# Image 0 in three transfers, TensorE sums part of the first cells, another split of tile 0

## The chip, the cores and the metric

The kernel runs on one core of one Trainium2 chip. Its time is the device time of one launch, in microseconds (us). A core has five engines with a queue of instructions each: TensorE (PE in the rows; PEld is its weight load), VectorE (DVE), ScalarE (ACT), GpSimd (POOL) and SyncE (SP), which here only issues DMA. They meet by semaphores.

## The reference

32 images of 96 channels, 56 by 56, fp32. The first layer scales every channel of every image by a gain that is computed from the data, the second is a depthwise masked 3x3 convolution whose four taps (left-up, up, right-up, left) are computed from the result of the first.

```python
# layer 0 (cut): which frequency each channel takes, from image 0 alone
g = relu(bn2(einsum('nchw,oc->nohw', x, wg1))).mean(axis=(2, 3))
xg0 = (relu(tanh(g @ wg2.T + bg2)) + beta)[0]
p_mid = round(xg0[:31] / xg0.sum() * 96)      # -> param, the edges of 32 channel ranges
filt = basis[i] where param[i] <= channel < param[i + 1]
# gain of each (image, channel): sums over a grid of 7 x 7 cells of 8 x 8 pixels
xp = x.reshape(n, c, 7, 8, 7, 8).mean(axis=(3, 5))
y = relu(bn1(sum(xp * filt) @ w1d[:, :, 1].T + b1d))
x = x * y[:, :, None, None] + x
# layer 1 (cut)
t = relu(bn(x.mean(axis=(2, 3)) @ w1.T))
wt = (t @ w2.T + b2).reshape(n * 96, 1, 3, 3) * mask   # 4 taps are left
out = depthwise_conv(x, wt, padding=1) + bias
```

## The kernel before

A tile is 128 rows (one image and channel each) of 3136 numbers; a group of three tiles is four whole images, and there are 8 groups, 24 tiles. SyncE loads tiles into nine buffers `xin` and stores them from four buffers `xout`. Tile k+9 is loaded when tile k has been computed.

**Steady state.** The rows of a tile are split among engines. VectorE computes the upper 27 rows (`tap`, three passes for the taps left-up, right-up and left; the tap up and the bias come with the seed, `seed_d` on ScalarE). TensorE computes the lowest 11 rows (`array_taps`, three products with the diagonal matrices `diag`) and two of the taps of the 18 rows between (`mixed_taps`); VectorE adds the last tap of those (`finish_mixed`, line 569). ScalarE seeds the sums, makes the diagonals and copies the 11 rows out. GpSimd does the left column of the result and folds a later tile to an eighth, which VectorE then sums to 49 cells. A product of TensorE in fp32 stands as two records in the trace. Beside this the coefficients of the next group are computed: `weigh_cells` on VectorE, then in turn `mix`, `hide`, `make_taps` and `spread_taps` on TensorE, with small steps of ScalarE and VectorE between them, and `coef_steps` at the end.

**Head.** Nothing can be convolved before the coefficients of group 0 are there. Three things lead to them, in this order on the engines:

1. The gate, from image 0. Its pixels come once more by DMA, into `image0` (a part of `xout`), in a layout of four quarters of 32 partitions each, by four transfers (line 287). `gate_w` holds the weights four times on its diagonal; GpSimd clears it and VectorE copies the blocks in (line 408). TensorE multiplies (line 698, six products of 392 columns), ScalarE applies batch norm and relu and sums (line 604), then a small product (701), tanh (607), `xg` (500), its sum (704), `counted` (507), `bounds` (707, 511), `hit` (515), `later` (710), `chosen` (521), `chosen_rows` (610) and the product `filt` (713) follow.
2. The cells of tiles 0, 1 and 2. VectorE reduces them directly (`sum_direct`, line 435) between the steps of the gate; GpSimd first folds 4 of the 7 cell rows of tile 1 and 3 of tile 2 in half (line 342, behind `counted`), and VectorE reduces the halves (line 442).
3. `weigh_cells(0)` (lines 464 to 470), then mix (721, 723), lift (619), total (477), hide (729), hidden (624), make_taps (735), gained (482), spread_taps (742) and `coef` (489, 494). VectorE reduces tile 3 in three pieces between them. Then it seeds its own rows of tile 0 (line 542), and the steady state begins.

`warm` (line 685) and line 689 are products with zeros; the former fill in where TensorE would stand still, the latter are needed once for each bank pair that is accumulated into. Lines 314 to 325 end the kernel with the stores of the last tile.

Of the kernel before, what the change touches and what calls it, by code (L numbers as in the profile page):

```python
# [33 lines left out]
VECTOR_ROWS, MIXED_ROWS, ARRAY_ROWS = 27, 18, 11  # L34
TOP_B = VECTOR_ROWS
TOP_A = VECTOR_ROWS + MIXED_ROWS
CHUNK_A = (ARRAY_ROWS + 1) // 2
CHUNK_B = (MIXED_ROWS + 1) // 2
BANK_A, BANK_B, BANK_D, BANK_S = 0, 2, 4, 7

# [3 lines left out]
HEAD_FOLDED = (0, 4, 3)  # L44
# [22 lines left out]
W_BIAS = 0  # L67
W_MIX = W_BIAS + PER
W_HIDE = W_MIX + PER * C
W_IDENT = W_HIDE + HID  # L70
W_IMAGE = W_IDENT + P
# [19 lines left out]

def build(nc, x, early, narrow, wide, out):
# [7 lines left out]
    x_image0 = x[0, :, :, :].rearrange("c h w -> c (h w)").rearrange("(q t) (j f) -> j q t f", t=PER, j=GROUP)  # L100

    with ExitStack() as ctx:
# [11 lines left out]
        gate_one = sb("gate_one", [QUAD, PER, E_END])  # L114
# [16 lines left out]
        edges = sb("edges", [P, 3, TOP_A])  # L131
# [34 lines left out]
        w_hid = wide_sb[0:C, W_HIDE:W_IDENT]  # L166
        ident = wide_sb[:, W_IDENT:W_IMAGE]
# [7 lines left out]
        acc_a = banks[:, BANK_A:BANK_B, :].rearrange("p b f -> p (b f)")[:, BANK - CHUNK_A * W:BANK + (ARRAY_ROWS - CHUNK_A) * W]  # L175
        acc_b = banks[:, BANK_B:BANK_D, :].rearrange("p b f -> p (b f)")[:, BANK - CHUNK_B * W:BANK + (MIXED_ROWS - CHUNK_B) * W]
        acc_d = banks[:, BANK_D:BANK_S, :].rearrange("p b f -> p (b f)")[:, 0:VECTOR_ROWS * W]
        gate_out = banks[:, BANK_A:BANK_B, :].rearrange("p b f -> p (b f)")[:, BANK - GATE_HALF:BANK + GATE_HALF]
        small = banks[:, BANK_S, :]
# [41 lines left out]
        image0_in = [sem(f"image0_in_{j}") for j in range(GROUP)]  # L221
# [4 lines left out]
        gate_zeroed = sem("gate_zeroed")  # L226
# [641 lines left out]
```

## Time and profile before

| | |
|---|---|
| median of three runs | 226.35 us (226.28 to 226.87) |
| profiled execution | 225.73 us, of which the span from first to last instruction is 223.9 us |
| busy: PE / DVE / POOL / ACT | 199.2 / 196.4 / 147.2 / 128.9 us |
| moved | 79.08 MB, 353 GB/s over the span |
| first tap of tile 0 | 36.0 us after the start |
| mean granted TensorE clock | 0.953 of 2.4 GHz |

All times in the rows count from the start of the span. The span has two parts: a head of 36 us, in which the engines wait for each other in a chain, and a steady part of 24 tiles at about 7.6 us, in which VectorE and TensorE are busy nearly all the time. The granted clock is 1.00 (2.4 GHz) in the steady part and changes between 1.00 and 0.50 (1.2 GHz) in the head.

### The profile page before, as it was taken

How to read it: one execution, taken by the hardware profiler on the slowest of the kernel's cores; microseconds unless marked ns; L12 is line 12 of the kernel's file. 1: busy time of each engine (PE TensorE's matmuls, PEld its weight loads, DVE VectorE, ACT ScalarE, POOL GpSimd, SP SyncE). 2: the span in 40 equal slices, each digit the busy share in tenths (PEclk: the TensorE clock that was granted, in tenths of full speed). 3: DMA queues.
4: the chain of work that ended last, by engine and by line, in shares of the span. 5: the costliest groups of instructions: out<-in, count | busy, mean ns of one | idle time of the engine just before them, and what ended most of it. 6: DMA issues, size and time to landing. Idle time of an engine off the chain costs nothing.

```text
span 223.9 us, 2408 instructions
## 1 busy us (share of the span) xinstructions
PE 199.2 (89%) x742; PEld 119.7 (53%) x742; DVE 196.4 (88%) x216; ACT 128.9 (58%) x190; POOL 147.2 (66%) x139
## 2 busy tenths in 40 slices
PE   7291775999999999999999999999999999999990
PEld 3141463556556565656664666466646654765540
DVE  6036969999999999999999999989999999988983
ACT  2002115638766867676867685768576857687640
POOL 3004267999999999999999999998999500040000
PEclk9769585999999999999999999999999999999999
DMA  4999999949999999999999999999997336625685
GB/s 112 279 426 418 430 428 425 395 155 332 421 426 405 419 426 426 408 397 430 430 422 408 428 426 428 408 423 426 423 406 325 148 143 287 287 108 215 254 332 241
DMA packets 8157, 79.08 MB, mean 353 GB/s; under 512 B 1040, under 2 KB 1072, under 8 KB 2128
## 3 DMA queue, kind: packets, MB, share of 16 engines
q1 hardware_dynamic: 8144, 78.92, 86.5%
q8 instruction: 6, 0.10, 0.2%
q14 instruction: 7, 0.06, 0.1%
HBM read 40.38 MB, written 38.54 MB: 352 GB/s over the span
## 4 chain that ended last, share of the span: by engine, by line
DVE 47%; PE 34%; issue 7%; ACT 5%; DMA 3%; SPq 1%; DVEq 1%; ACTq 0%
DVE banks L560 23%; PE banks L750 23%; DVE xout L560 8%; DVE xout L569 7%; PE banks L698 3%; ACT banks L635 3%; DMA xout<-x 3%; PE banks L735 2%; PE banks L742 2%; DVE stats L442 2%; DVE sums L467 1%; PE banks L685 1%; DVE stats L448 1%; DVE stats L435 1%; DVE stats L464 1%
## 5 line engine op out<-in xcount | busy, mean ns | idle before, releaser
L750 PE MATMUL banks<-xin,diag 128*128 128x330 f32 (+2 forms) x480 | 162.5, 492 | 2.9 <-ACT banks L635 2.9
L750 PEld LDWEIGHTS banks<-xin,diag 128*128 128x128 f32 x480 | 89.5, 192 | 58.0 <-issue 36.6
L635 ACT ACTIVATE banks<-xin,wide_sb,coef 128x616 f32<-128x616 f32 (+2 forms) x71 | 84.4, 1208 | 21.3 <-DVE xout L560 10.7
L342 POOL TENSOR_TENSOR halves<-xin 128x1568 f32<-128x1568 f32 (+2 forms) x22 | 74.1, 3370 | 23.2 <-DVE count L507 14.7
L560 DVE SCALAR_TENSOR_TENSOR banks<-xin,coef,banks 128x1485 f32<-128x1485 f32 x48 | 84.8, 1767 | 4.8 <-ACT banks L635 4.2
L560 DVE SCALAR_TENSOR_TENSOR xout<-xin,coef,banks 128x1485 f32<-128x1485 f32 x24 | 42.2, 1758 | 0.6 <-issue 0.3
L347 POOL TENSOR_TENSOR halves<-halves 128x784 f32<-128x784 f32 x18 | 33.2, 1846 | 1.4
L569 DVE SCALAR_TENSOR_TENSOR xout<-xin,coef,banks 128x990 f32<-128x990 f32 x24 | 29.8, 1243 | 2.5 <-PE banks L750 2.5
L630 ACT ACTIVATE diag<-wide_sb,coef 128x128 f32<-128x128 f32 x72 | 23.4, 389 | 9.7 <-DVE coef L494 9.7
L656 ACT ACTIVATE xout<-banks 128x616 f32<-128x616 f32 x24 | 16.4, 682 | 17.6 <-PE banks L750 16.7
L374 POOL TENSOR_TENSOR edges<-xin,coef 128x90 f32<-128x90 f32 x24 | 8.3, 347 | 19.0 <-DVE coef L494 19.0
L352 POOL TENSOR_TENSOR rows<-halves 128x392 f32<-128x392 f32 x18 | 18.3, 1019 | 1.4
L435 DVE TENSOR_REDUCE stats<-xin 128x14 f32<-128x896 f32 (+3 forms) x9 | 11.0, 1227 | 7.7 <-DMA xin<-x 7.7
L698 PE MATMUL banks<-xout,gate_w 128*128 128x392 f32 x12 | 6.8, 747 | 4.1 <-DMA xout<-x 4.1
L448 DVE TENSOR_REDUCE stats<-rows 128x49 f32<-128x392 f32 x18 | 10.0, 554 | 0.0
L604 ACT ACTIVATE banks<-banks,b_gate,a_gate 128x784 f32<-128x784 f32 x1 | 1.0, 977 | 14.7 <-PE banks L698 14.7
L624 ACT ACTIVATE hidden<-banks,b_hid,a_hid 32x4 f32<-32x4 f32 x8 | 2.8, 346 | 11.4 <-PE banks L729 11.4
L735 PEld LDWEIGHTS banks<-hidden,narrow_sb 32*96 32x96 f32 x64 | 6.0, 159 | 5.6 <-issue 5.1
L721 PEld LDWEIGHTS banks<-by_image,wide_sb 128*96 128x96 f32 x48 | 5.0, 175 | 5.4 <-DVE by_image L470 4.2
L379 POOL TENSOR_TENSOR xout<-edges,wide_sb 128x45 f32<-128x45 f32 x24 | 6.6, 273 | 1.9
L377 POOL TENSOR_TENSOR edges<-edges 128x45 f32<-128x45 f32 x24 | 6.2, 260 | 1.9
L698 PEld LDWEIGHTS banks<-xout,gate_w 128*128 128x128 f32 x12 | 3.4, 297 | 7.5 <-issue 7.2
(73 smaller groups left out, 88.4 us busy)
## 6 DMA issues: line engine op xcount, KB each, us to landing
xin<-x SPq DMA_DIRECT2D x23, 1568.0 KB, 9.7
out<-xout SPq DMA_DIRECT2D x23, 1568.0 KB, 11.7
xout<-x SPq DMA_DIRECT2D x4, 294.0 KB, 5.1
xin<-x SPq DMA_DIRECT2D x1, 1120.0 KB, 14.5
out<-xout SPq DMA_DIRECT2D x1, 756.0 KB, 3.2
out<-xout SPq DMA_DIRECT2D x1, 504.0 KB, 3.3
wide_sb<-wide SPq DMA_DIRECT2D x1, 499.5 KB, 15.8
xin<-x SPq DMA_DIRECT2D x1, 448.0 KB, 15.1
```

The costliest lines, as they stand in the source:

```text
L342: eng.tensor_tensor(halves[:, j % 2, 0:end, :], cells[:, :, 0, :], cells[:, :, 1, :], ALU.add).then_inc(once_folded, 1)
L347: eng.tensor_tensor(cells[:, :, 0, :], cells[:, :, 0, :], cells[:, :, 1, :], ALU.add).then_inc(twice_folded, 1)
L352: eng.tensor_tensor(rows8[:, j % 2, :].rearrange("p (a f) -> p a f", a=DCT), cells[:, :, 0, :], cells[:, :, 1, :], ALU.add).then_inc(thric ...
L435: return vec.tensor_reduce(cells_of(j, first, end), xin[:, j % IN_BUFS, PAD + first * BLK * W:PAD + end * BLK * W].rearrange("p (a b c d) ...
L448: return vec.tensor_reduce(stats[:, 0, j % PER, :], rows8[:, j % 2, :].rearrange("p (c d) -> p c d", d=BLK), AX.X, ALU.add)
L560: return vec.scalar_tensor_tensor(out=to, in0=grid(k)[:, irows, cols], scalar=weight(k, which), in1=d_rows[:, :, ocols], op0=ALU.mult, op1 ...
L569: vec.scalar_tensor_tensor(out=result(k)[:, TOP_B:TOP_A, ocols], in0=grid(k)[:, irows, cols], scalar=weight(k, LEFT), in1=b_rows[:, :, ocols],
L630: ins = sca.activation(diag[:, k % 2, which, :], ident, ACT.Copy, scale=weight(k, which))
L635: return sca.activation(acc, above_rows(k, first, end), ACT.Identity, bias=bias[:, k % PER:k % PER + 1], scale=weight(k, UP))
L656: sca.activation(xout[:, k % OUT_BUFS, TOP_A * W:], acc_a, ACT.Copy).then_inc(a_out, 1)
L698: ins = mm(gate_out[:, part], gate_w[:, t, :], image0[:, t, part], start=(t == 0), stop=(t == PER - 1))
L750: return mm(to, diag[:, k % 2, which, :], grid(k)[:, irows, cols], start=False, stop=(which == LEFT), skip_group_check=True)
```

## The change

- **Image 0** comes in three transfers, one for each channel of three, each to all 128 partitions (a channel in four quarters on four neighbouring partitions). The first products wait only for the first transfer. `gate_w` is now made by three VectorE multiplications of the gate's weights, which come spread over 128 partitions, with a 0/1 matrix `quarter_of`; GpSimd's clearing and the four copies go.
- **Parameters.** `early_sb` and `narrow_sb` are issued by ScalarE, ahead of its table load. The array `wide` is split: its first 132 columns (`quarter_of` and `ident`) come ahead of image 0, the rest where all of it came before.
- **Cells.** TensorE adds the eight pixel rows of a cell row up, by eight accumulating products with the identity (`sum_cells`), for 4, 4, 3 and 2 of the 7 cell rows of tiles 0 to 3; VectorE reduces what is left, one eighth of the numbers (`sum_array`). Before, these were direct reductions in tiles 0 and 3 and reductions of halves in tiles 1 and 2. GpSimd's two folds of the head go. VectorE's direct sum of four cell rows of tile 0 ahead of `xg` goes.
- **TensorE's filling**: 4 products with zeros ahead of the gate where there was 1, 2 behind it, two for the second bank pair ahead of `s_mm`, 1 behind `s_mm`, 1 between mix and hide; the 2 ahead of mix go.
- **Tile 0** is split 20/18/18 rows. ScalarE seeds the array rows of tile 0 before it makes the diagonals, and each diagonal is signalled by itself. The sums of VectorE's rows start 8 numbers later in their banks.

```diff
+ROWS = (27, 18, 11)
+FIRST_ROWS = (20, 18, 18)
+ARRAY_CELLS = ((0, 4), (0, 4), (0, 3), (0, 2))
...
         def _(sp):
-            sp.dma_start(early_sb[:, :], early[:, E_GATE2:E_END]).then_inc(early_in, 16)
-            sp.dma_start(gate_one[:, :, :], early.rearrange("(q t) e -> q t e", t=PER)).then_inc(gate_one_in, 16)
-            for j in range(GROUP):
-                sp.dma_start(image0[QUAD * j:QUAD * (j + 1), :, :], x_image0[j]).then_inc(image0_in[j], 16)
-            sp.dma_start(narrow_sb[:, :], narrow).then_inc(narrow_in, 16)
+            sp.dma_start(gate_one[:, :], early.rearrange("(q j t) e -> q j (t e)", j=1, t=PER).broadcast_to(
+                [QUAD, GROUP, PER * E_END])).then_inc(gate_one_in, 16)
+            sp.dma_start(wide_sb[:, 0:W_BIAS], wide[:, 0:W_BIAS]).then_inc(ident_in, 16)
+            for t in range(PER):
+                sp.dma_start(image0[:, t, :], x_image0[t]).then_inc(image0_in[t], 16)
...
-            pool.wait_ge(loaded[1], 16)
-            pool.wait_ge(counted, 1)
-            fold_once(1, HEAD_FOLDED[1])
-            pool.wait_ge(part_in, 16)
-            fold_once(2, HEAD_FOLDED[2])
...
-            dve.wait_ge(loaded[0], 16)
-            sum_direct(0, 0, 4)
             dve.wait_ge(gate_tanh, 1)
             vec.tensor_scalar(xg[:, :], gate_act[:, :], 0.0, gate_par[0:NF, 5:6], ALU.max, ALU.add).then_inc(xg_done, 1)
-            sum_direct(0, 4, 5)
...
+            sum_array(0).then_inc(cells_done, 1)
+            dve.wait_ge(loaded[1], 16)
+            sum_direct(1, 4, DCT)
+            sum_array(1).then_inc(cells_done, 1)
             dve.wait_ge(part_in, 16)
-            sum_direct(2, HEAD_FOLDED[2], HEAD_PART)
+            sum_direct(2, 3, HEAD_PART)
             dve.wait_ge(loaded[2], 16)
             sum_direct(2, HEAD_PART, DCT)
-            sum_once_folded(2, 2, HEAD_FOLDED[2]).then_inc(cells_done, 1)
+            sum_array(2).then_inc(cells_done, 1)
...
+            def sum_cells(j, begin, stop):
+
+                first, end = ARRAY_CELLS[j]
+                cells = xin[:, j % IN_BUFS, PAD:].rearrange("p (a b f) -> p a b f", a=DCT, b=BLK)
+                for b in range(begin, stop):
+                    ins = mm(array_cells_of(j), ident, cells[:, first:end, b, :],
+                             start=(b == 0), stop=(b == BLK - 1))
```

On TensorE, from its first instruction to the sum of `xg` (`prime` is L689 and L746, `warm` L685 and L730, the gate L698 and L756). Before:

```order
L689 MATMUL banks<-zeros 128x512 x2
L685 MATMUL banks<-zeros 128x392
L698 MATMUL banks<-xout,gate_w 128x392 x6
L701 MATMUL banks<-gate_sum,gate_in 32x1
L704 MATMUL banks<-xg,narrow_sb 32x1
```

and in the changed kernel:

```order
L746 MATMUL banks<-zeros 128x512 x2
L730 MATMUL banks<-zeros 128x392 x4
L756 MATMUL banks<-xout,gate_w 128x392 x6
L730 MATMUL banks<-zeros 128x392 x2
L760 MATMUL banks<-gate_sum,gate_in 32x1
L746 MATMUL banks<-zeros 128x512 x2
L764 MATMUL banks<-xg,narrow_sb 32x1
L730 MATMUL banks<-zeros 128x392
```

Three more wide products with zeros stand ahead of the gate, two behind it, and two ahead of the sum of `xg`.

On TensorE, from `bounds` to mix. Before:

```order
L707 MATMUL banks<-count,narrow_sb 32x1 x2
L710 MATMUL banks<-hit,narrow_sb 32x96
L713 MATMUL banks<-narrow_sb,chosen_rows 128x49 x3
L685 MATMUL banks<-zeros 128x392 x2
L721 MATMUL banks<-by_image,wide_sb 96x4 x3
L723 MATMUL banks<-by_image,wide_sb 96x4 x3
```

and in the changed kernel, where L737 is `sum_cells`:

```order
L768 MATMUL banks<-count,narrow_sb 32x1 x2
L737 MATMUL banks<-xin,wide_sb 128x224 x3
L773 MATMUL banks<-hit,narrow_sb 32x96
L737 MATMUL banks<-xin,wide_sb 128x224 x5
L777 MATMUL banks<-narrow_sb,chosen_rows 128x49 x3
L737 MATMUL banks<-xin,wide_sb 128x224 x8
L737 MATMUL banks<-xin,wide_sb 128x168 x8
L785 MATMUL banks<-by_image,wide_sb 96x4 x3
L787 MATMUL banks<-by_image,wide_sb 96x4 x3
```

The products `later` (L773) and `filt` (L777) now stand behind 3 and 5 wide ones in the same queue, and mix behind 16.

On TensorE, from hide to the products of tile 0. Before:

```order
L729 MATMUL banks<-total,wide_sb 32x4
L735 MATMUL banks<-hidden,narrow_sb 96x4 x4
L742 MATMUL banks<-taps,wide_sb 128x16 x3
L750 MATMUL banks<-xin,diag 128x6x55 x3
L750 MATMUL banks<-xin,diag 128x5x55 x3
```

and in the changed kernel:

```order
L730 MATMUL banks<-zeros 128x392
L793 MATMUL banks<-total,wide_sb 32x4
L737 MATMUL banks<-xin,wide_sb 128x112 x3
L799 MATMUL banks<-hidden,narrow_sb 96x4 x4
L737 MATMUL banks<-xin,wide_sb 128x112 x2
L806 MATMUL banks<-taps,wide_sb 128x16 x3
L737 MATMUL banks<-xin,wide_sb 128x112 x3
L814 MATMUL banks<-xin,diag 128x9x55 x10
```

The cells of tile 3 stand in three pieces between the narrow products, and the products of tile 0 are 9 rows each.

## Rows read from the trace of the kernel before

**Rows 1.** Chain that ended last, in order of time: start us, us, what.

```profile
3.65 6.23 DMA xout<-x
...
10.02 6.86 PE banks L698 x12
...
16.97 1.10 ACT banks L604 x2
...
31.14 0.85 PE banks L735 x8
...
34.12 1.86 DVE banks L542
...
57.12 3.43 PE banks L750 x8
```

**Rows 2.** Windows: stretch, busy us (instructions) by engine, granted clock, DMA share, GB/s.

```profile
5.20:8.50 3.30, 0.71 (x3) 0.08 (x1) 0.79 (x8) 0.00 (x0) 0.10 (x1) 1.00 1.06 218
8.60:10.00 1.40, 0.00 (x0) 0.01 (x1) 0.00 (x0) 0.00 (x0) 0.00 (x0) 0.50 1.07 282
...
12.00:15.00 3.00, 3.00 (x6) 1.62 (x5) 1.16 (x1) 0.00 (x0) 0.00 (x0) 0.50 0.98 414
15.50:18.50 3.00, 1.59 (x7) 0.59 (x5) 0.36 (x1) 1.22 (x3) 0.00 (x0) 1.00 1.01 424
18.50:22.00 3.50, 0.80 (x8) 0.46 (x8) 3.19 (x10) 0.13 (x1) 1.98 (x1) 1.00 1.02 413
22.50:28.50 6.00, 4.65 (x12) 2.78 (x12) 5.80 (x10) 0.70 (x2) 1.16 (x1) 0.50 1.00 429
29.10:32.30 3.20, 1.81 (x19) 1.55 (x18) 1.93 (x5) 0.70 (x2) 2.08 (x1) 1.00 1.00 424
32.50:35.50 3.00, 1.03 (x6) 0.92 (x5) 2.47 (x4) 1.32 (x4) 2.72 (x2) 0.50 0.97 410
36.00:39.00 3.00, 2.93 (x6) 1.90 (x7) 2.99 (x2) 1.04 (x1) 2.32 (x4) 0.50 1.02 425
39.50:44.00 4.50, 4.50 (x15) 2.56 (x14) 4.46 (x3) 3.02 (x6) 4.31 (x2) 1.00 0.99 421
```

**Rows 3.** TensorE's timeline: start us, us, instructions merged.

```profile
1.45 3.78 PE L689 MATMUL banks<-zeros 128*128 128x512 f32 x4 [1.45 <-DVE zeros L395]
5.02 0.88 PE L685 MATMUL banks<-zeros 128*128 128x392 f32 x2
...
23.85 1.51 PE L713 MATMUL banks<-narrow_sb,chosen_rows 32*128 32x49 f32 x6 [1.83 <-ACT chosen_rows L610]
...
36.07 9.86 PE L750 MATMUL banks<-xin,diag 128*128 128x330 f32 x26 [2.54 <-ACT banks L635]
```

**Rows 4.** DMA issues of the whole span: count, KB each, median us to landing.

```profile
xout<-x SPq DMA_DIRECT2D x4, 294.0 KB, 5.1
...
wide_sb<-wide SPq DMA_DIRECT2D x1, 499.5 KB, 15.8
```

**Rows 5.** VectorE's timeline.

```profile
19.73 0.14 DVE L507 TENSOR_SCALAR count<-share 32x1 f32<-32x1 f32 x1
...
21.54 1.53 DVE L435 TENSOR_REDUCE stats<-xin 128x21 f32<-128x1344 f32 x1
...
27.11 0.31 DVE L464 TENSOR_TENSOR stats<-stats,banks 128x147 f32<-128x147 f32 x1
...
27.95 0.18 DVE L470 TENSOR_TENSOR by_image<-sums,banks 128x24 f32<-128x24 f32 x1
...
36.01 1.77 DVE L560 SCALAR_TENSOR_TENSOR banks<-xin,coef,banks 128x1485 f32<-128x1485 f32 x1
...
45.61 1.24 DVE L569 SCALAR_TENSOR_TENSOR xout<-xin,coef,banks 128x990 f32<-128x990 f32 x1
...
52.56 1.25 DVE L569 SCALAR_TENSOR_TENSOR xout<-xin,coef,banks 128x990 f32<-128x990 f32 x1
```

**Rows 6.** Who waited for whom, whole span: us in total, times, longest us.

```profile
DVE xout L569 <- PE banks L750: 2.5, 7, 0.7
```

More of the change, by code:

```diff
@@ L89, with split, top_b, top_a @@
 S_END = S_ABOVE + C
+def split(k):
+    return FIRST_ROWS if k == 0 else ROWS
+def top_b(k):
+    return split(k)[0]
+def top_a(k):
+    return top_b(k) + split(k)[1]
+def top_p(k):
+    return top_a(k) + split(k)[2]
+def chunks(rows):
+    return [(0, (rows + 1) // 2), ((rows + 1) // 2, rows)]
 def build(nc, x, early, narrow, wide, out):
@@ L220, in build @@
         wide_in = sem("wide_in")
-        image0_in = [sem(f"image0_in_{j}") for j in range(GROUP)]
+        image0_in = [sem(f"image0_in_{t}") for t in range(PER)]
+        ident_in = sem("ident_in")
+        array_cells = sem("array_cells")
         part_in = sem("part_in")
@@ L225, in build @@
         zeroed = sem("zeroed")
-        gate_zeroed = sem("gate_zeroed")
         gate_placed = sem("gate_placed")
@@ L396, in _ @@
             vec.memset(xin[:, :, 0:PAD], 0.0).then_inc(pad_zeroed, 1)
+            dve.wait_ge(gate_one_in, 16)
+            dve.wait_ge(ident_in, 16)
+            for t in range(PER):
+                vec.tensor_tensor(gate_w[:, t, :].rearrange("p (j o) -> p j o", j=GROUP),
+                                  gate_one[:, E_END * t:E_END * t + NF].rearrange("p (j o) -> p j o", j=1).broadcast_to(
+                                      [P, GROUP, NF]),
+                                  quarter_of.rearrange("p (j o) -> p j o", o=1).broadcast_to([P, GROUP, NF]),
+                                  ALU.mult).then_inc(gate_placed, 1)
             dve.wait_ge(early_in, 16)
@@ L437, in sum_direct, with sum_array, sum_once_folded @@
                                              "p (a b c d) -> p a c b d", b=BLK, c=DCT, d=BLK), AX.XY, ALU.add)
-            def sum_once_folded(j, folds, end=DCT):
-                dve.wait_ge(once_folded, folds)
-                return vec.tensor_reduce(cells_of(j, 0, end), halves[:, j % 2, 0:end, :].rearrange(
+            def sum_array(j):
+                first, end = ARRAY_CELLS[j]
+                dve.wait_ge(array_cells, j + 1)
+                return vec.tensor_reduce(stats[:, 0, j % PER, first * DCT:end * DCT],
+                                         array_cells_of(j).rearrange("p (c d) -> p c d", d=BLK),
+                                         AX.X, ALU.add)
+            def sum_once_folded(j):
+                dve.wait_ge(once_folded, j - ONCE[0] + 1)
+                return vec.tensor_reduce(cells_of(j), halves[:, j % 2, :, :].rearrange(
                     "p a (b c d) -> p a c b d", c=DCT, d=BLK), AX.XY, ALU.add)
@@ L558, in tap @@
                         dve.wait_ge(stored[k % OUT_BUFS], 16 * (k // OUT_BUFS))
-                to = result(k)[:, 0:VECTOR_ROWS, ocols] if which == LEFT else d_rows[:, :, ocols]
+                acc = acc_d(k, first, end).rearrange("p (r c) -> p r c", c=W)[:, :, ocols]
+                to = result(k)[:, first:end, ocols] if which == LEFT else acc
                 return vec.scalar_tensor_tensor(out=to, in0=grid(k)[:, irows, cols], scalar=weight(k, which),
-                                                in1=d_rows[:, :, ocols], op0=ALU.mult, op1=ALU.add)
+                                                in1=acc, op0=ALU.mult, op1=ALU.add)
             def finish_mixed(k):
-                irows, cols, ocols = window(TOP_B, TOP_A, LEFT)
+                irows, cols, ocols = window(top_b(k), top_a(k), LEFT)
                 dve.wait_ge(conv_b, k + 1)
@@ L598, in _ @@
             sca = nc.scalar
+            sca.dma_start(early_sb[:, :], early[:, E_GATE2:E_END]).then_inc(early_in, 16)
+            sca.dma_start(narrow_sb[:, :], narrow).then_inc(narrow_in, 16)
             act.wait_ge(zeroed, 1)
@@ L753, in array_taps @@
             def array_taps(k, chunk):
-                for which in (LEFT_UP, RIGHT_UP, LEFT):
-                    ins = add_tap(k, acc_a, TOP_A, *[(0, CHUNK_A), (CHUNK_A, ARRAY_ROWS)][chunk], which)
+                for n, which in enumerate((LEFT_UP, RIGHT_UP, LEFT)):
+                    if k == 0 and chunk == 0:
+                        pe.wait_ge(diag_done, n + 1)
+                    ins = add_tap(k, acc_a(k), top_a(k), *chunks(top_p(k) - top_a(k))[chunk], which)
                 return ins
```

154 lines of the change are left out of this document (86 added, 68 removed).

## The prediction

> **What bounds the kernel now.** I read the chain that ended last first, since it says what the end hangs on. For the first 36 us it goes from engine to engine and hardly any work is parallel on it: image 0 lands at 3.65 + 6.23 = 9.88, TensorE multiplies it until 16.88, ScalarE's relu follows, and the coefficients are there just before the seed at 34.12 [rows 1]. From then on it is VectorE and, in stretches, TensorE: the last piece shown, eight products of 495 columns that end at 60.55, is TensorE's, and VectorE waited for TensorE ahead of line 569 seven times, 2.5 us in all [rows 6]. So in the steady part two engines are nearly level, and what the head gains moves everything behind it, as long as TensorE comes forward as much as VectorE does.
>
> Then the windows, for TensorE's clock [rows 2]. It is granted 1.00 (2.4 GHz) until 8.5, 0.50 (1.2 GHz) from 8.6, 1.00 again from 15.5 to 22, 0.50 to 28.5, 1.00 to 32.3, 0.50 to 39, and then 1.00 to the end. Most of the gate ran at the low clock.
>
> Prices of TensorE, in records (two for a product). At 2.4 GHz eight records of 495 columns take 3.43 us, of which some 0.13 is the tail of the last one, so 0.83 ns a column [rows 1]. The records of 512 columns at the start (four from 1.45 to 5.02) come to 0.89 us each, 1.74 ns a column [rows 3]: in fact the low clock, although the window says 1.00 there. A narrow record costs its weights and not its columns: 49 columns 1.51 / 6 = 0.25 us at 1.2 GHz [rows 3], so 0.125 at 2.4, and 4 columns 0.85 / 8 = 0.105 at 2.4 [rows 1].
>
> **The gate.** Removed: the wait for image 0 until 9.88. The four transfers to 32 partitions each took 5.1 us (median), at 218 to 282 GB/s with the DMA share above 1 [rows 2, 4]. Transfers to 128 partitions run at 414 to 429 GB/s, the rest of `wide` with 4 KB a partition among them [rows 2, 4]. The three new ones are 1.2 MB: 2.8 us at the high rate, after what is queued ahead they land by about 7; at the old rate by 9.9. Neither is late, since TensorE comes to the gate later than that: its four records of 512 end at 4.9, the eight of 392 behind them take 8 x 0.33 = 2.6 at 2.4 GHz, so it begins at 7.6, and needs the third channel only at 7.6 + 8 x 0.33 = 10.2. `gate_w` is three VectorE multiplications of 128x128 (0.31 each by the 128x147 one, rows 5) once its parameters land, at about 3.5, and done by 4.7. No cost; nor have the two issues on ScalarE's queue, which put its table load off by about 1 us, with relu 8 us later, nor the second part of `wide`, which goes out where all of it went. The gate is then 12 x 0.33 = 3.9 us without a break in TensorE's work and ends at 11.5, where it ended at 16.88. That is 5.4 us, the largest single gain, and most of it is given back in the next part.
>
> **From relu to the filter.** Relu takes 1.10 [rows 1]: 12.7. Two warm products (1.3 us) lie beside it. The gate's second product, then two products of 512 columns, 4 x 0.43 = 1.7, which end at 14.8, while tanh and `xg` are ready at 13.6: 1.2 us of new delay. The small steps keep their length (count is 0.14, rows 5), here as below: sum, share and count end at 15.7. The direct sum that stood ahead of `xg` (0.5) is gone, so is GpSimd's fold. `bounds` ends at 16.15, `hit` at 17.0 (VectorE, 0.8 us). Now the cells of TensorE stand in the queue: 224 columns are 0.187 us a record, so 6 records 1.1 us up to 17.2, `later` until 17.4; VectorE is in its direct sum until 18.0, `chosen` 18.25, `chosen_rows` 18.8; the other 10 records of tile 0 end at 19.2, `filt` at 20.0 (6 x 0.125). Tile 1 follows, 16 x 0.187 = 3.0, until 23.0, and tile 2, 16 x 0.14 = 2.2, until 25.2. Tiles 1 and 2 landed in time for that even before. VectorE has 1344 numbers of tile 1 (1.53 us, rows 5) and 1792 of tile 2 (2.0) to add directly and comes to the same point at 25.3. With 0.25 for the last reduction of an eighth and 1.0 for weighing, `by_image` is ready at 26.6, against 27.95 + 0.18 = 28.13 [rows 5]. **Gain so far 1.5 us.** TensorE is now the chain here; the loads have 1 to 3 us of air.
>
> **From mix to the first tap**, at 2.4 GHz. Mix 12 x 0.108 = 1.3, until 27.9; the warm product (0.65) hides lift and total. Hide ends at 28.75, hidden 29.1; six records of tile 3's cells (6 x 0.125) end at 29.5 and hold make_taps back by 0.4; 0.85 [rows 1] makes 30.35. `gained`, four more records, spread 6 x 0.125: 31.6, coefficients at 32.1. Before, spread ran at the low clock, and this is where the 0.5 more comes from: gain 2.0. Then the last 6 records and a reduction of an eighth stand ahead of VectorE's seed, 0.3 us of cost, and the seed of 20 rows is 1.86 x 20/27 = 1.38, 0.48 less. The first tap starts at 33.9, against 36.01 [rows 5]: 2.1.
>
> **Tile 0.** Three taps of 20 rows instead of 27: 3 x 1.73 x 7/27 = 1.3 us less on VectorE. It is ready for `finish_mixed(0)` at 45.61 - 2.1 - 1.3 = 42.2. TensorE pays for that: 20 records of 495 columns are 9900 columns instead of 7590, 8.2 us. Seed first and the diagonals one by one let it start at 33.7 (it started at 36.07), so it ends at 42.0, just in time. Then tile 1: the two halves of its array rows, mix between them (1.3), four records of 495, hide and four more, by the same prices 7.9 us: 49.9. VectorE would be there at 49.3 and was there at 52.56 [rows 5]. So here TensorE ends last, and of VectorE's 3.4 us **2.6 stay**. ScalarE, with 18 rows to copy out instead of 11 (0.4 us), has the seed for VectorE's next tile at 43.3 and is wanted at 43.4; that is worth 0 to 0.3. From here the two kernels have the same instructions. GpSimd's folds of tiles 4 and 5 wait only for the loads and are ready 2 us ahead; loads and stores move with the tiles.
>
> Sum: 1.5 + 0.5 + 0.1 + 1.3 - 0.8 = 2.6 us. The profiled execution would be 225.73 - 2.6 = 223.1 (a span of 221.3), and that execution lies 0.62 below the median, so against the median 226.35 the forecast is **223.7**.
>
> **What the sum rests on: the clock.** Everything above has 2.4 GHz from 5.1 us on. Up to 25 us TensorE is busy with wide products nearly all the time, and in the rows such work lifted the clock or held it (12 to 15, then 15.5 to 18.5). From 25.2 to 33.7 it is not: narrow products and waits, with 0.65 us of a warm product and 1.5 us of cells between them. Three rows bracket that. From 29.1 to 32.3 TensorE was busy 1.81 of 3.20 us, all with products of 4 and 16 columns, and the clock fell behind it; from 5.2 to 8.5 it had 0.71 us of mostly wide work and then stood still, and it fell too; from 15.5 to 18.5, with some 1.4 us of wide work, it held [rows 2]. The changed kernel lies between these, and no row tells on which side. I give about even.
>
> The Trainium skill ("TensorE: Matmul & The Clock Gate", section "HAM oscillation — how this bites in real kernels") puts the loss of the clock down to waits in which TensorE stands idle. By that rule alone the clock would hold here and the time would be the forecast. The fall behind 32.3 came after narrow work with short waits only, so this trace does not bear it out.
>
> **Rivals.**
> 1. *The clock falls at about 29 or 32 and stays low into tile 0.* Slower side. Make_taps costs 0.85 more, the remaining cells and spread 1.5 more, so coefficients at 34.3; the last six records 0.75 more, the first tap at 36.9. In the trace the clock came back only at about 39.3, behind 36.0 to 39.0 of wide products [rows 2]. TensorE then has its first 2.5 us of tile 0 at 1.2 GHz, ends it at about 46.3, and 7.9 later stands at 54.2 where VectorE was at 52.56: +1.7, 228.0. If the clock falls only behind 32, the products from 33.7 to 39.3 are low, some 7 records, 2.8 us: 44.8 + 7.9 = 52.7, and with the last cells of tile 3 +0.4, 226.8. It decides from six low records of tile 0 on, since each costs 0.41 and 6 x 0.41 eats the 2.6. For: the brackets above, and that before, the clock was low in exactly this place. Against: the new wide products between the narrow ones.
> 2. *It falls and comes back at once*, since the half clock makes the cells twice as long and TensorE fuller. Some 3 us at 1.2 GHz in one of the two places cost 1.2 to 1.7 us: 224.9 to 225.4.
> 3. *The early clock comes late*, or is lost once between 8 and 19. Each product of 392 columns costs 0.65 more. If half the filling and the first gate products run low, 1.6 us go: 225.3. Against: the first 3.6 us are the same work as before.
> 4. *TensorE is not late in tile 1*, and all of VectorE's 3.4 us stay: 222.9. Against it stands that the chain already ran over TensorE there.
>
> That the new transfers are no faster is no rival: the gate does not wait for them.
>
> **Numbers.** Chances: forecast 0.47 (own range 223.2 to 224.3), rival 1 0.25, rival 2 0.16, rival 3 0.08, rival 4 0.04. A measurement of this kernel can tell about 0.3% from no change, 0.7 us: faster is below 225.7. That is the forecast, rival 4 and most of rivals 2 and 3: 0.71. Of rival 1, 0.10 lies within 0.3% (225.7 to 227.0), with the rest of 2 and 3 0.14; slower is 0.15. Range 222.8 to 227.1: it leaves out the worse half of rival 1 and a little below.
>
> **What would show it.** Right: gate products end near 11.5, `by_image` at 26.6, first tap at 33.9, the second line-612 instruction (`finish_mixed(1)`) at 49.9 behind TensorE, clock 1.00 throughout from 5.1. Wrong: a window at 0.50 between 25 and 39; a gate that waits for image 0; `by_image` later than 27; or TensorE's tile 0 ending behind VectorE's.

## The result, and the profile of the changed kernel

The changed kernel is slower: 229.69 us (median of 4 runs, 229.52 to 230.25) against 226.61 (226.28 to 228.56) on the same chip, a ratio of 1.014 with a 95% interval of 1.008 to 1.019. The forecast was 223.7 with a range up to 227.1. The time lies beyond that range, on the side of rival 1. Ratios and intervals here leave out executions over 1.5% above the fastest of the same kernel; where such executions are themselves the finding, all times are listed.

The profiled execution took 229.56 us with a span of 227.7 (before: 225.73 and 223.9). Three lines of its page, the busy times, the granted clock in 40 slices and the shares of the chain:

```profile
PE 214.9 (94%) x820; PEld 132.3 (58%) x820; DVE 191.3 (84%) x215; ACT 129.6 (57%) x190; POOL 143.9 (63%) x136
...
PEclk9999955899999999999999999999999999999998
...
PE 52%; DVE 38%; issue 6%; ACT 2%; DVEq 1%; ACTq 0%
```

TensorE is busy 16 us more than before, VectorE 5 us less: work has gone to the engine that now holds half of the chain (the page gives `sum_cells`, L737, 13.6 us). And the clock has a hole in slices 6 to 8. Windows, in the columns of [rows 2], show its edges:

```profile
27.50:28.00 0.50, 0.32 (x4) 0.35 (x5) 0.50 (x2) 0.00 (x0) 0.00 (x0) 1.00 0.95 401
28.00:28.50 0.50, 0.50 (x6) 0.50 (x6) 0.50 (x1) 0.00 (x0) 0.00 (x0) 0.70 0.94 401
28.50:41.50 13.00, 12.14 (x43) 9.01 (x44) 6.05 (x10) 3.88 (x7) 7.78 (x5) 0.50 1.01 427
41.50:42.00 0.50, 0.50 (x2) 0.12 (x1) 0.50 (x1) 0.00 (x0) 0.00 (x0) 0.65 0.93 393
```

The granted clock goes to 0.50 (1.2 GHz) at about 28.2 and comes back at about 41.8. From 28.5 to 41.5 TensorE is busy for 12.1 of 13 us, and from 27.68 to 37.61 without a break, so the work it had did not bring the clock back soon. The chain that ended last, in order of time (start us, us, what), answers to [rows 1]:

```profile
7.47 3.95 PE banks L756 x12
...
15.81 0.21 PE banks L768 x4
16.02 1.33 PE banks L737 x6
...
17.63 2.09 PE banks L737 x10
19.72 0.79 PE banks L777 x6
20.51 3.24 PE banks L737 x16
...
23.77 0.39 DVE stats L479
24.17 1.98 DVE stats L471 x2
...
27.36 0.19 DVE by_image L514
...
28.33 0.96 PE banks L787 x6
29.29 1.51 PE banks L730 x2
...
31.00 1.55 PE banks L737 x6
32.55 1.37 PE banks L799 x8
33.92 1.12 PE banks L737 x4
35.05 1.13 PE banks L806 x6
...
38.47 11.88 PE banks L814 x26
```

The gate (L756) ends at 11.42, where it ended at 16.88. Of the 16.1 us from there to `by_image` at 27.54 `sum_cells` (L737) has 6.7; from 28 to 36 the chain is TensorE at 1.2 GHz: a product of zeros 1.51, the cells of tile 3 and `make_taps` (L799) 1.37, where the latter had 0.85 [rows 1]. Two rows, one of TensorE's timeline and one of VectorE's, stand on either side of the fall:

```profile
27.68 0.64 PE L785 MATMUL banks<-by_image,wide_sb 128*96 128x4 f32 x6 [1.67 <-DVE by_image L514]
...
33.96 0.17 DVE L526 SCALAR_TENSOR_TENSOR taps<-lift,banks 96x16 f32<-96x16 f32 x1 [3.04 <-PE banks L799]
```

TensorE stood still for 1.67 us ahead of mix, which the two products of zeros had filled before; then VectorE waited 3.04 us for `make_taps`. What remains in the steady part is one offset. VectorE's last tap of the mixed rows (L612 now, L569 before), tiles 0 to 2:

```profile
48.72 1.25 DVE L612 SCALAR_TENSOR_TENSOR xout<-xin,coef,banks 128x990 f32<-128x990 f32 x1 [0.94 <-PE banks L814]
...
56.49 1.25 DVE L612 SCALAR_TENSOR_TENSOR xout<-xin,coef,banks 128x990 f32<-128x990 f32 x1 [0.77 <-PE banks L814]
...
64.51 1.25 DVE L612 SCALAR_TENSOR_TENSOR xout<-xin,coef,banks 128x990 f32<-128x990 f32 x1 [0.26 <-PE banks L814]
```

They waited for TensorE each time. The second stood at 52.56 before [rows 5], so 3.93 us are lost by then, and 3.8 us is what the spans differ by. The whole loss is made ahead of 57 us.

### The profile page after: what moved, and what is told of

Same layout as the page of the kernel before. It is cut to its first block, busy times and chain, and to the rows that moved or that the text cites. A ratio compares the mean times of both kernels' runs of the same rounds, so it can differ in the third digit from the quotient of the medians.

```text
span 227.7 us, 2556 instructions
## 1 busy us (share of the span) xinstructions
PE 214.9 (94%) x820; PEld 132.3 (58%) x820; DVE 191.3 (84%) x215; ACT 129.6 (57%) x190; POOL 143.9 (63%) x136
## 4 chain that ended last, share of the span: by engine, by line
PE 52%; DVE 38%; issue 6%; ACT 2%; DVEq 1%; ACTq 0%
PE banks L814 33%; DVE banks L603 18%; DVE xout L612 7%; DVE xout L603 6%; PE banks L737 4%; PE banks L799 3%; PE banks L730 3%; PE banks L746 2%; PE banks L806 2%; ACT banks L679 2%; PE banks L756 2%; DVE sums L511 1%; DVE stats L492 1%; DVE stats L508 1%; DVE stats L471 1%
## 5 line engine op out<-in xcount | busy, mean ns | idle before, releaser
L814 PE MATMUL banks<-xin,diag 128*128 128x495 f32 (+2 forms) x480 | 164.5, 496 | 1.3 <-ACT diag L675 0.9
L679 ACT ACTIVATE banks<-xin,wide_sb,coef 128x1008 f32<-128x1008 f32 (+2 forms) x71 | 84.8, 1213 | 25.0 <-DVE xout L603 10.3
L381 POOL TENSOR_TENSOR halves<-xin 128x1568 f32<-128x1568 f32 x20 | 70.4, 3520 | 28.1 <-DMA xin<-x 22.7
L603 DVE SCALAR_TENSOR_TENSOR banks<-xin,coef,banks 128x1485 f32<-128x1485 f32 (+1 forms) x48 | 84.0, 1751 | 4.8 <-ACT banks L679 4.2
L603 DVE SCALAR_TENSOR_TENSOR xout<-xin,coef,banks 128x1485 f32<-128x1485 f32 (+1 forms) x24 | 41.8, 1741 | 0.4
L612 DVE SCALAR_TENSOR_TENSOR xout<-xin,coef,banks 128x990 f32<-128x990 f32 x24 | 29.9, 1244 | 4.4 <-PE banks L814 4.4
L700 ACT ACTIVATE xout<-banks 128x616 f32<-128x616 f32 (+1 forms) x24 | 16.7, 696 | 20.0 <-PE banks L814 19.3
L407 POOL TENSOR_TENSOR edges<-xin,coef 128x90 f32<-128x90 f32 (+1 forms) x24 | 8.3, 348 | 19.0 <-DVE coef L538 18.2
L737 PE MATMUL banks<-xin,wide_sb 128*128 128x224 f32 (+2 forms) x64 | 13.6, 369 | 0.0
L737 PEld LDWEIGHTS banks<-xin,wide_sb 128*128 128x128 f32 x64 | 11.9, 225 | 0.2
L799 PEld LDWEIGHTS banks<-hidden,narrow_sb 32*96 32x96 f32 x64 | 6.6, 173 | 5.3 <-issue 5.3
L471 DVE TENSOR_REDUCE stats<-xin 128x14 f32<-128x896 f32 (+2 forms) x7 | 7.9, 1140 | 0.0
```

Of the source, the lines that this page charges most:

```text
L381: eng.tensor_tensor(halves[:, j % 2, :, :], cells[:, :, 0, :], cells[:, :, 1, :], ALU.add).then_inc(once_folded, 1)
L603: return vec.scalar_tensor_tensor(out=to, in0=grid(k)[:, irows, cols], scalar=weight(k, which), in1=acc, op0=ALU.mult, op1=ALU.add)
L612: vec.scalar_tensor_tensor(out=result(k)[:, top_b(k):top_a(k), ocols], in0=grid(k)[:, irows, cols], scalar=weight(k, LEFT), in1=acc_b(k).r ...
L679: return sca.activation(acc, above_rows(k, first, end), ACT.Identity, bias=bias[:, k % PER:k % PER + 1], scale=weight(k, UP))
L700: sca.activation(xout[:, k % OUT_BUFS, top_a(k) * W:top_p(k) * W], acc_a(k), ACT.Copy).then_inc(a_out, 1)
L737: ins = mm(array_cells_of(j), ident, cells[:, first:end, b, :], start=(b == 0), stop=(b == BLK - 1))
```

## The experiments

Two theories came first. **Clock**: without the two products of zeros ahead of mix TensorE's clock falls at 28, and all of the loss is narrow and wide products at 1.2 GHz. **Load**: too much work went to TensorE (cells, 18 rows of tile 0 instead of 11), and it is last whatever the clock. Each run is set against the kernel before on its own chip: 226.02 us (11 runs) for the first four, 226.07 (19) for the next four, 226.13 (19) for the last four.

### Filling put back ahead of mix (e1_fill2)

```diff
             sum_cells(2, 0, BLK)
+            for _ in range(2):
+                mm(banks[:, BANK_B, 0:392], zeros[:, 0:P], zeros[:, 0:392], start=True, stop=True)
             pe.wait_ge(wide_in, 16)
```

The two products write over what L746 had prepared in that bank pair, which changes values of tile 0; no instruction is left out.

> The changed kernel with two products of 392 columns with zeros behind the cells of tile 2, ahead of mix, in the 1.67 us in which TensorE stood still there (26.02 to 27.68). They are 1.3 us at 2.4 GHz, so they cost at most 0.1 us by themselves. Clock theory: the granted clock no longer falls at 28.2 but stays 1.00 up to tile 0, coefficients at about 33.3 instead of 36.7, tile 0's products 3 us shorter; 225.0 (224.0 to 226.0), 3.5 to 5 us faster than the changed kernel. Load theory (TensorE simply has too much to do: cells and 18 rows of tile 0): no change or up to 0.5 us slower than 229.7.

225.64 us (225.10 to 226.05, 8 runs), ratio 0.9985 (0.9968 to 1.0002): 3.5 us back by the ratios, 4.0 by the medians, and level with the kernel before, as the clock theory had it. A window of this kernel:

```profile
29.00:38.00 9.00, 7.44 (x51) 5.70 (x52) 6.32 (x10) 3.89 (x7) 7.79 (x5) 1.00 1.00 424
```

and, from its VectorE timeline, the second L612:

```profile
52.57 1.25 DVE L612 SCALAR_TENSOR_TENSOR xout<-xin,coef,banks 128x990 f32<-128x990 f32 x1 [0.78 <-PE banks L819]
```

The clock is at 1.00 all through, and VectorE is at this point at 52.57, where the kernel before was at 52.56 [rows 5]. So the clock is the whole loss against before. But the gate ended at 12.73 here against 16.88, and of those 4.2 us nothing is left either. That became the second question.

The gate ended at 11.42 in the changed kernel's trace, 1.3 earlier than here, although nothing ahead of it differs. The opening products with zeros took longer here. First the changed kernel, then e1:

```profile
4.67 2.80 PE L730 MATMUL banks<-zeros 128*128 128x392 f32 x8
...
5.03 3.76 PE L730 MATMUL banks<-zeros 128*128 128x392 f32 x8
```

So two traces are best compared from a common point on, here from `by_image`.

### The split of tile 0 taken back (e2_split27)

```diff
-FIRST_ROWS = (20, 18, 18)
+FIRST_ROWS = (27, 18, 11)
...
             dve.wait_ge(coef_done, 1)
+            dve.wait_ge(cells_done, PER + 1)
```

> The changed kernel with tile 0 split 27/18/11 again (and one more wait of VectorE on itself). Load theory: TensorE's 2310 columns less of tile 0 take 1.9 us (3.8 at the low clock) off a chain that ends on it, so 1 to 3 us faster than the changed kernel: 227 to 228.5. Clock theory: with the clock still low until 42, VectorE has 1.8 us more and comes to be last; 229.5 to 230.8, the same to 1 us slower.

230.22 us (229.52 to 230.92, 4 runs), ratio 1.0185 (1.015 to 1.022). The clock was low from 31.0 to 41.2. The head was late as in e1 (`by_image` at 28.91 against 27.54), so the stretch behind it is what compares: from `by_image` to the second last tap of the mixed rows it takes 28.96 us, in the changed kernel 28.95. Taking 2310 columns off TensorE made it no faster, since VectorE, which got the seven rows, came to be last in tile 0. The load theory, which wanted 1 to 3 us here, falls.

### No cells of tile 3 on TensorE (e3_nocells3)

```diff
-            sum_direct(PER, 2, 5)
+            sum_direct(PER, 0, 3)
...
-            pe.wait_ge(loaded[PER], 16)
-            sum_cells(PER, 0, 3)
             make_taps(0)
-            sum_cells(PER, 3, 5)
             spread_taps(0)
-            sum_cells(PER, 5, BLK)
```

> The changed kernel without TensorE's sums of tile 3: VectorE adds all seven cell rows of tile 3 directly, as before. TensorE has 16 records less among the narrow products, 4.4 us at 1.2 GHz, of which about 1.2 + 0.9 us stood ahead of make_taps and spread. Load theory: 2 to 4 us faster, 226 to 227.5. Clock theory: the clock falls at 28.2 all the same, the records save what stood ahead of the narrow products, and VectorE's direct sums fill the waits: 1 to 2.5 us faster, 227.2 to 228.7, with 0.50 granted up to tile 0.

228.29 us (227.94 to 228.83, 4 runs), ratio 1.010 (1.008 to 1.012): better than the changed kernel by 0.8 us by the ratios and 1.4 by the medians. That is in the range of the clock theory and not in that of the load theory. The fall is there all the same, from 30.2 to 40.5, but fewer products stand in it: from `by_image` (28.56) to the second last tap (55.05) it takes 26.49 us, 2.5 less than the changed kernel. The cells of tile 3 cost that much at the low clock, or somewhat less, since it fell 1.7 us behind `by_image` here and 0.7 in the changed kernel. So the load is not nothing, but it is less than the clock, which gave e1 5.2 us over the same stretch.

### The kernel before without its filling (e4_b_nowarm)

```diff
-            warm(2)
             pe.wait_ge(wide_in, 16)
```

> The kernel before without its two products with zeros ahead of mix (2.9 us of TensorE's idle time at 1.2 GHz). Clock theory: the clock, which rose at 29.0 behind them, now stays at 0.50 from 22.3 to about 39; mix, make_taps and half of spread cost twice, 1.0 to 1.8 us slower than before (0.5% to 0.8%). Load theory: no change, or 0.2 us faster, since TensorE has less to do.

227.79 us (227.51 to 227.98, 4 runs), ratio 1.0076 (1.006 to 1.009). Removing the same two products costs the other kernel 1.7 us. Its chain:

```profile
28.66 1.10 PE banks L721 x6
...
32.11 1.45 PE banks L735 x8
...
33.81 1.48 PE banks L742 x6
...
37.81 10.86 PE banks L750 x26
```

The clock stayed at 0.50 from 22.5 to 43.0, and `make_taps` took 1.45 where it took 0.85 [rows 1]. The 26 records of L750 took 10.86 instead of 9.86 [rows 3]. Here the filling lifts a clock that is already low, in the changed kernel it would have held a high one; in both it is worth more than it costs.

### The preparing products as filling (e5_move_prime, e6_move_warm2)

The two products of 512 columns that the bank pair needs stood ahead of `s_mm`, in the chain. In e5 they move into the idle time ahead of mix; e6 has two products of zeros ahead of the gate instead of four as well.

```diff
-            prime(BANK_A)                   # ahead of s_mm
...
             sum_cells(2, 0, BLK)
+            prime(BANK_A)
             pe.wait_ge(wide_in, 16)
...
-            warm(4)                         # e6 only
+            warm(2)
```

> The changed kernel with its two products of 512 columns for the second bank pair moved from ahead of the sum of xg into TensorE's idle time ahead of mix. One move, nothing added. Clock theory with the delay of 1.2 us that the prediction named: the clock holds as in the run with two added products, and sum, count and all cells behind them come 1.2 to 1.5 us earlier; 224.0 to 224.8, about 1.2 us faster than with the added products and 5 us faster than the changed kernel. Rival (the delay ahead of the sum was hidden, since TensorE's cells or the loads set the pace): 225.6 as with the added products.

Ten runs, in two or three heaps rather than around one value, so neither expectation fits: four lie below both, six above. Each execution has its mean granted clock:

| us | mean clock |
|---|---|
| 223.32, 223.78, 223.84, 223.85 | 0.996 to 0.997 |
| 226.05, 226.65, 226.80, 226.87, 227.23 | 0.984 to 0.988 |
| 228.49 | 0.976 |

The median is 226.35, no gain on the kernel before (226.07); without the four slowest the ratio is 0.992 (0.987 to 0.998). One kernel, one chip, and 5 us between its executions, in the order of the clock. That fits the clock theory without a second kernel, but it is a correlation, and no trace of a slow execution was kept. In the profiled execution (223.78 us, clock 1.00 throughout) the preparing products are out of the way:

```profile
19.99 5.50 PE banks L737 x32
25.49 1.72 PE banks L746 x4
...
34.37 10.20 PE banks L813 x26
```

`by_image` is ready at 27.01 there, 1.85 us earlier than in e1. The gate ended 0.64 earlier (12.09), and the other 1.2 are what the move was expected to give.

> As the run before, and two products with zeros ahead of the gate instead of four (1.3 us at 2.4 GHz, 2.6 at 1.2). If the gate waits for these and not for image 0, it begins up to 1.3 us earlier and the whole comes 0.7 to 1.3 us earlier: 223.2 to 224.0. If image 0 is what it waits for, or the loads of tiles 1 and 2 set the pace behind it, no change to the run before.

225.43 us (223.24 to 226.96, 10 runs), ratio 0.9955 (0.991 to 0.9997), slower than expected. Again the fastest run, 223.24, has 0.996 and the four from 226.04 on 0.976 to 0.977. In the profiled run (226.25) the gate did begin 1.3 earlier (6.81 against 8.14). TensorE went into mix without idle time and the clock still fell, at 29.5, until 39.8. Idle time ahead of mix is therefore not the only thing that loses it: here it was lost among the narrow products behind mix.

### Tile 0 at 22/18/16 rows (e7_rows22), and more wide work behind mix (e12_wide_cells3)

```diff
-FIRST_ROWS = (20, 18, 18)
+FIRST_ROWS = (22, 18, 16)                      # e7, on top of e6
...
-ARRAY_CELLS = ((0, 4), (0, 4), (0, 3), (0, 2))
+ARRAY_CELLS = ((0, 4), (0, 4), (0, 3), (0, 4)) # e12, on top of e7
```

> As the run before, with tile 0 split 22/18/16 rows. TensorE has 2 rows x 3 taps less in tile 0, 660 columns or 0.55 us, VectorE 0.36 us more. If TensorE is the one that ends last from tile 0 to tile 2, 0.3 to 0.5 us faster than the run before; if VectorE is, 0.3 us slower.

223.38 us (222.87 to 224.24, 4 runs), ratio 0.990 (0.986 to 0.993). That is 2.0 below the median of e6, where the split was expected to give 0.5 at most, so the split's own work does not account for most of it; e6 by itself scatters by 3.7. In the profiled execution (224.24, the slowest of the four) the clock was low from 34.5 to 37.9 only. It fell among the wide products of tile 0, behind a stretch of 1.46 us in which TensorE stood still.

> The version with 22/18/16 rows (223.4) with TensorE summing 4 cell rows of tile 3 instead of 2: 16 records of 224 columns instead of 112 between the narrow products, 0.20 us each instead of 0.14 at 2.4 GHz. 6 records more time 0.07 us stand ahead of make_taps (0.4 us) and 4 ahead of spread (0.25). If the clock of that stretch is what scatters the times, these runs lie close together (within 1 us) at 223.2 to 224.2; if it is not, they are 0.6 us slower than with the narrow ones and scatter as much.

223.88 us (223.40 to 224.27, 4 runs), ratio 0.988 (0.982 to 0.994), mean clock 0.992 to 0.997. With products of 224 columns instead of 112 between the narrow ones it held in the profiled run:

```profile
29.00:38.00 9.00, 8.03 (x38) 5.50 (x37) 5.55 (x8) 3.09 (x5) 7.43 (x4) 1.00 1.01 425
```

The four runs lie within 0.9 us, but those of e7, with the narrower products, lie within 1.4, and the time is that of e7. Four runs each do not show that the width of these products is what held the clock.

### The gate's part alone (e8_gate_alone)

Image 0 in three transfers, the parameters, four products of zeros ahead of the gate and two behind it, and ScalarE's order of work in tile 0, as in the changed kernel. The preparing products ahead of `s_mm` and the single products of zeros behind `s_mm` and mix go. Cells, the split of tile 0 and the filling ahead of mix as in the kernel before.

```diff
-FIRST_ROWS = (20, 18, 18)
+FIRST_ROWS = (27, 18, 11)
...
-            sum_cells(0, 0, 3)
...
-            sum_cells(0, 3, BLK)
...
-            sum_cells(1, 0, BLK)
-            sum_cells(2, 0, BLK)
+            warm(2)
             pe.wait_ge(wide_in, 16)
```

> The new gate alone: image 0 in three transfers, gate_w by multiplication, parameters on ScalarE's queue, four filling products ahead and two behind the gate; cells, split of tile 0 and the two products ahead of mix as in the kernel before. Theory (TensorE's cells eat what the gate gains): the gate ends near 11.5 to 12.7, by_image is ready 2.5 to 4 us earlier than in the kernel before (28.1) and most of it stays: 222.5 to 224.5. Rival (loads and VectorE's sums set the pace anyway, the gate's gain is worth little by itself): 225.0 to 226.3.

223.37 us (222.97 to 223.88, 4 runs), ratio 0.989 (0.987 to 0.992): 2.7 us faster than before, with the clock low from 17.5 to 38.0. The chain:

```profile
3.92 9.73 DMA xin<-x
13.68 2.02 DVE stats L478
...
20.79 1.51 PE banks L779 x6
...
25.21 1.09 PE banks L787 x6
...
32.41 1.87 DVE banks L593
```

`by_image` is ready at 25.07, against 28.13 before [rows 5] and 28.86 in e1, whose gate ended at nearly the same time (12.88 here, 12.73 there). Only the cells, and what stands around them, lie between the two. Here the chain begins with the load of tile 0, which lands at 13.65 and whose sum on VectorE holds `xg` back to 15.70; and VectorE waited 1.00 us for tile 3:

```profile
26.07 1.55 DVE L478 TENSOR_REDUCE stats<-xin 128x21 f32<-128x1344 f32 x1 [1.00 <-DMA xin<-x]
```

So the loads are the next bound.

### How much of the gate's part is the clock (e9_b_fill_gate)

The kernel before with one edit, eight products of zeros ahead of the gate:

```diff
-            warm(1)
+            warm(8)
             pe.wait_ge(gate_placed, GROUP)
```

> The kernel before with one edit: eight products of 392 columns with zeros ahead of the gate instead of one, which keep TensorE busy from 5.0 to about 9.9 to 10.5, when image 0 lands in its four transfers. If the gate's gain is the clock's (it ran 10.0 to 15.4 at 1.2 GHz), the gate takes 4.0 us instead of 6.9 and ends at 14, VectorE's sums begin with tile 0's landing at 13.8 either way, and by_image is ready about 2.5 to 3 us earlier: 223.0 to 224.3, the same as the new gate alone. If the gain is that of the three transfers, it stays at 225.5 to 226.5.

224.54 us (224.20 to 226.46, 10 runs), ratio 0.992 (0.988 to 0.995). The gate, in the chain of the profiled run:

```profile
11.68 3.96 PE banks L698 x12
```

3.96 us instead of 6.86 [rows 1]. It started 1.66 later, behind the filling, which was sized too long, and ended 1.24 earlier. This execution took 226.46 us and is the slowest of the ten (the others lie between 224.20 and 224.64), so its trace is used for the gate alone. The time lies between the two expectations: by the medians 1.6 of the 2.7 us of e8 come from seven wide products alone, by the ratios 1.9 of 2.4. What is left, 0.6 to 1.1, belongs to the rest of e8 (the transfers and the earlier start that they allow, `gate_w`, the parameters, the products behind the gate), which was not taken apart.

### What the cells and the split add to it (e10_gate_cells0, e11_gate_split)

e10 is e8 with the cells of tile 0 on TensorE, e11 is e8 with 20/18/18 rows and the preparing products as the filling ahead of mix.

```diff
+            pe.wait_ge(loaded[0], 16)          # e10
+            sum_cells(0, 0, 3)
             pe.wait_ge(hit_done, 1)
...
+            sum_cells(0, 3, BLK)
...
-FIRST_ROWS = (27, 18, 11)                      # e11
+FIRST_ROWS = (20, 18, 18)
-            warm(2)
+            prime(BANK_A)
             pe.wait_ge(wide_in, 16)
```

> The new gate alone (223.4 in the run before) with TensorE summing the first 4 cell rows of tile 0 (16 records of 224 columns, 3.2 us at 2.4 GHz) instead of VectorE (1.95 us), the reduction of an eighth (0.3 us) behind chosen. VectorE has 1.6 us less between tile 0's landing and by_image; TensorE has idle time there, but later and filt stand behind the wide products. If VectorE's work is what paces this stretch, by_image is 0.5 to 1.5 us earlier and the total 222.0 to 223.2; if the queueing on TensorE eats it, 223.4 to 224.5.

224.98 us (223.16 to 226.85, 10 runs), ratio 0.992 (0.988 to 0.996). The median is 1.6 above e8, above both expected ranges, and nine of the ten executions are slower than the slowest of e8 (223.88). But the times go with the clock again, from 223.16 at 0.965 to 226.85 at 0.941. The trace is of the slowest execution. In it ten records of the cells stand ahead of `filt`, at 1.2 GHz, and `by_image` is ready at 28.05, where e8 had it at 25.07:

```profile
18.70 4.04 PE banks L743 x10
```

So the cells of tile 0 cost time here, and how much of it at full clock is not settled.

> The new gate alone with tile 0 split 20/18/18, the two products of 512 columns for the second bank pair in place of the two of 392 ahead of mix. VectorE gains 1.8 us of tile 0, TensorE has 1.9 us more at 2.4 GHz and 3.8 at 1.2. In the run before, TensorE's clock was 0.50 until 38. Theory (TensorE then ends last in tile 0 and 1, the split is a loss): 223.8 to 225.5. Rival (the split is a gain that the cells alone had spoilt): 221.8 to 223.0.

223.97 us (223.05 to 225.56, 4 runs), ratio 0.989 (0.982 to 0.995). The last step to the coefficients starts at 31.31, 0.86 earlier than in e8, and nothing of it arrives. TensorE's first stretch of tile products in the chain, and the first L619 in VectorE's timeline:

```profile
33.27 11.91 PE banks L816 x26
```

```profile
43.55 1.25 DVE L619 SCALAR_TENSOR_TENSOR xout<-xin,coef,banks 128x990 f32<-128x990 f32 x1 [2.04 <-PE banks L816]
```

VectorE is ready 2.04 us before TensorE has the rows. The second L619 starts at 51.32, in e8 at 50.85. The split moves the wait from one engine to the other.

## Why the prediction was wrong

**The step that failed is the one on the clock.** The prediction had named the place ("a window at 0.50 between 25 and 39"), the mechanism, and the sign, as rival 1 with a chance of 0.25. Two things made that chance too low.

First, it never priced the wait ahead of mix. Its own numbers have one: TensorE ends the cells at 25.2 and `by_image` comes at 26.6. It counted this into "narrow products and waits" without asking what the two removed products had covered. The trace shows cells ending at 26.0, `by_image` at 27.54, and 1.67 us in which TensorE stood still; e1 fills them and gets the loss back, e4 takes the filling out of the other kernel and loses 1.7. The diff had this edit in a line of its own, and the prediction cost it at nothing. The Trainium skill ("TensorE: Matmul & The Clock Gate", section "HAM oscillation — how this bites in real kernels") puts the loss of the clock down to waits in which TensorE stands idle. e1 agrees with it: without the wait of 1.67 us the clock held. But the waits of the page's own case are for DMA and longer than this one, so the page did not tell the outcome either, and in e6 the clock fell without a wait ahead of mix.

Second, once low the clock stayed low for 13.6 us (28.2 to 41.8), as rival 1 said, with TensorE busy 12.1 of the 13 us shown above; rival 2 (back at once because TensorE is fuller) did not occur. Rival 3, an early clock that comes late, did not occur in the changed kernel's trace, but in e1's, where it moved the gate's end by 1.3 us.

**Where the 6.6 us lie.** At the second L612 the prediction had 49.9 and the trace 56.49. By stage:

| | predicted | trace | e1, clock at 1.00 |
|---|---|---|---|
| gate ends | 11.5 | 11.42 | 12.73 |
| `by_image` ready | 26.6 | 27.54 | 28.86 |
| from there to `coef` ready | 5.5 | 9.18 | 5.60 |
| from there to the first L612 | 10.1 | 12.00 | 10.33 |
| from there to the second L612 | 7.7 | 7.77 | 7.78 |

The prices of the last three stages were right within 0.3 us each at 2.4 GHz. The low clock added 3.6 (9.18 - 5.60) and 1.7 (12.00 - 10.33), 5.3 in all; e1 began 1.3 later, which leaves the 3.9 to 4.0 between the two kernels. Of the remaining 1.3 of the miss 0.9 is in the stage ahead of `by_image` and 0.4 in those small differences.

**That stage, rows that were mis-sized.** A record of 224 columns was worked out at 0.187 us from the price of a column and takes 3.24 / 16 = 0.2025; over the 32 records of tiles 0 and 1 that is 0.5 us. Each sum of an eighth was put at 0.25, and those of 224 numbers took 0.39. The rest is in small steps, such as 0.28 for `later` and 1.1 instead of 1.0 for weighing. The order was right: VectorE waited for the cells of tile 1 (2.17 us), and its direct sums of tile 2 came behind them, at 1.98 where the prediction had 2.0.

**Rival 1's own size.** It gave 228.0, with the second L612 at 54.2, 2.3 too early. Of that 0.9 is the stage above. It had 7.7 us from `by_image` to the coefficients (26.6 to 34.3) where the trace has 9.18: 1.5 more, since it let the clock fall 2.4 us behind `by_image`, behind mix and the product of zeros, and it fell 0.7 behind. From the coefficients to the first L612 it had 12.0 (34.3 to 46.3), and that is what the trace shows.

**What held.** The gate did not wait for image 0; the transfers took 4.1 us each where they took 5.1 [rows 4]:

```profile
xout<-x SPq DMA_DIRECT2D x3, 392.0 KB, 4.1
```

The two 512-column products did stand in the chain ahead of the sum of `xg`, where VectorE waited 1.58 us for that sum, and e5 shows what it is worth to move them. TensorE ended last in tile 1. In the head of the changed kernel neither TensorE nor VectorE waited for a tile's load, so there was air in the loads, as predicted. It is small: GpSimd had tile 4 at 29.89, where in the kernel before it had it at 30.22, so earlier transfers of image 0 brought the loads behind them forward by about 0.3 us, and in e8, whose `by_image` is 2.5 us earlier than the changed kernel's, VectorE waited for tiles 0 and 3. With two products of zeros fewer ahead of the gate, in e12, TensorE did wait for image 0, which landed at 9.32:

```profile
3.29 6.03 DMA xout<-x
```

**Why the gate's 4 to 5 us bring nothing in the changed kernel even at full clock.** The exchange of work is bad. Four of the seven cell rows of a tile cost VectorE 2.02 us directly (`DVE stats L478` in e8, 1792 numbers). On TensorE they are 3.24 us of its queue and 0.39 of VectorE's. With nearly the same end of the gate the product `filt` ends at 22.30 in e8 and at 21.83 in e1, so the cells up to there cost little; not nothing, since e8 was at 1.2 GHz there and `filt` alone took it 0.7 longer (1.51 against 0.79). Behind it `by_image` takes 2.8 us in e8 and 7.0 in e1: the 16 records of tile 1's cells stand in the queue there (21.83 to 25.07), then the reduction, and then the direct sums of tile 2, which e8 has nearly done by that time. That the exchange is the cause rests on these two traces; e10, meant to split it by tile, points the same way but mixes it with the clock. With the preparing products out of the chain and the idle time filled (the four fastest runs of e5, e7, e12) the cells on TensorE come to 223.3 to 223.9, which is the time of e8 without any of them.

What stays open: the parameters on ScalarE's queue and the new `gate_w` were never changed by themselves. Nor is it settled which of idle time, narrowness and the phase of earlier work decides the clock in an execution of e5. e8 still ran 20 us of its head at 1.2 GHz; a version with its gate and the clock held through mix was not tried.

Best of the kernels run: e8 (223.37), e7 (223.38) and e12 (223.88), each 1.0 to 1.2% faster than the kernel before and not told apart by these runs.

## What to carry to other kernels

Products of zeros are part of the time, not decoration: before removing one, look at what TensorE does in that gap without it, and price everything behind the gap at 1.2 GHz until the clock comes back. Work moved to an idle engine has to be priced there in that engine's time and in its place in the queue; here 2.0 us of VectorE became 3.2 us of TensorE ahead of the next link of the chain. Test a bundle of edits in parts: one of these was worth 2.7 us and the others took it away.

## What the runs showed of the hardware

- The granted clock differs between executions of one program on one chip: 223.32 to 228.49 us in e5, at a mean clock of 0.997 to 0.976. The kernel before has it too, 225.35 us at 0.953 and 228.29 at 0.927, though one of its executions took 227.32 at 0.958, so not all scatter is the clock. A kernel whose head lies near the edge needs ten runs, and the profiled one may be of either kind.
- A low clock was not soon cured by being busy: 12.1 busy us of 13 in the changed kernel before it rose, and the two products of zeros in e8 (2.91 us at 22.3, at 1.2 GHz) did not lift it, while the same two in the kernel before ended with it at 1.00 from 29.1 on [rows 2]. In e11 two of 512 in the same place (3.71 us at 22.3) were followed by 1.00 from 26.5 to 29.9.
- The first products with zeros ran at the low speed although the clock is given as 1.00 there: four records of 512 columns took 3.38 us in the changed kernel and 3.78 in the kernel before [rows 3], and 1.72 in e5 at 25.49. When the full speed came differed: eight records of 392 behind them took 2.80 us in the changed kernel and 3.76 in e1.
